# Softmax inverse row sums and output weights of a post-norm transformer block: from TensorE transposes to DMAs

## The reference

```python
x = layernorm(x + attention(x, w_qkv, b_qkv, w_out, b_out))   # 16 heads of width 32, causal softmax
x = layernorm(x + ffn(x))                                      # gate/up/down of width 2048, int weights minus 128, row scales
# attention: softmax(q k^T / sqrt(32) + causal) v, then  out @ w_out.T + b_out
# ffn: Wg = (gate_w - 128) * gate_scale[:, None] and so on;  (silu(x Wg^T) * (x Wu^T)) Wd^T
```

## Time and profile before

| | us |
|---|---|
| three executions: median (lowest, highest) | 734.27 (732.36, 735.01) |
| the profiled execution | 732.33 |
| its span, first to last instruction | 730.5 |
| mean granted TensorE clock, share of full | 0.996 |
| PE busy | 711.2 (97%) |
| DVE, ACT, POOL busy | 386.0, 373.1, 187.0 |

### The profile page before, as it was taken

How to read it: one execution, slowest core, us unless ns; L and a number is a source line. 1 busy time by engine, 2 the same in 40 slices (tenths; PEclk the granted TensorE clock), 3 DMA queues, 4 the chain that set the end, 5 groups by cost and what they waited for, 6 DMA issues and landing times.

```text
span 730.5 us, 11735 instructions
## 1 busy us (share of the span) xinstructions
PE 711.2 (97%) x4368; PEld 551.7 (76%) x4368; DVE 386.0 (53%) x988; ACT 373.1 (51%) x900; POOL 187.0 (26%) x198
## 2 busy tenths in 40 slices
PE   7999899999999999999999999999999999999994
PEld 6777577777777677776688888888888888888883
DVE  4766576666667665577552322553344533544335
ACT  3676676767776776777765653322232222322230
POOL 0011610347132660418833233221020002000004
PEclk9999999999999999999999999999999999999998
DMA  9821453346741577314688964852321013000111
GB/s 306 222 79 30 87 135 126 87 98 143 204 135 59 123 168 235 75 39 116 154 179 162 209 148 145 219 193 79 144 70 45 0 43 129 0 1 1 57 59 59
DMA packets 97207, 83.35 MB, mean 114 GB/s; under 512 B 64128, under 2 KB 73344, under 8 KB 97024
## 3 DMA queue, kind: packets, MB, share of 16 engines
q1 hardware_dynamic: 90624, 62.69, 30.8%
q0 software_dynamic: 6528, 19.93, 12.1%
HBM read 59.53 MB, written 22.02 MB: 112 GB/s over the span
## 4 chain that ended last, share of the span: by engine, by line
PE 92%; POOL 4%; DVE 2%; issue 1%; DMA 1%; ACT 0%; POOLq 0%; SPq 0%; DVEq 0%
PE bank L1506 16%; PE bank L1507 16%; PE bank L1293 12%; PE bank L1372 9%; PE bank L1514 7%; PE bank L1513 7%; PE bank L1311 6%; PE bank L1355 5%; PE bank L1330 5%; PE bank L1393 5%; POOL z_tok L684 1%; PE bank L1404 1%; PE bank L1259 1%; POOL xT_lo L717 1%; DVE probs L1048 1%; POOL z_tok L810 1%
## 5 line engine op out<-in xcount | busy, mean ns | idle before, releaser
L840 ACT ACTIVATE probs<-probs,neg_max 128x128 f32<-128x128 f32 (+3 forms) x256 | 140.3, 552 | 3.0 <-DVE neg_max L1048 2.9
L1048 DVE CUSTOM_DVE_ANT_0 probs<-bank,causal 128x128 f32<-128x128 f32 (+3 forms) x256 | 111.7, 484 | 41.2 <-PE bank L1355 41.2
L1166 DVE SCALAR_TENSOR_TENSOR hid<-bank,u_scale,silu 128x512 f32<-128x512 f32 x64 | 48.0, 750 | 157.2 <-PE bank L1507 156.0
L1506 PE MATMUL bank<-xT_hi,gateT 128*128 128x512 f32 x256 | 99.7, 389 | 0.0
L1507 PE MATMUL bank<-xT_lo,gateT 128*128 128x512 f32 x256 | 99.6, 389 | 0.0
L1506 PE MATMUL bank<-xT_hi,upT 128*128 128x512 f32 x256 | 99.6, 389 | 0.0
L1507 PE MATMUL bank<-xT_lo,upT 128*128 128x512 f32 x256 | 99.6, 389 | 0.0
L1372 PEld LDWEIGHTS bank<-ident,probs 128*128 128x128 f32 x640 | 71.5, 140 | 35.0 <-issue 24.2
L948 ACT ACTIVATE silu<-bank,g_scale 128x512 f32<-128x512 f32 x64 | 44.0, 688 | 102.2 <-PE bank L1507 102.2
L898 ACT ACTIVATE probsT<-bank 128x512 f32<-128x512 f32 x80 | 47.7, 596 | 92.0 <-PE bank L1372 90.1
L954 ACT ACTIVATE hid_hi<-hid 128x512 fp32r<-128x512 f32 x58 | 36.7, 632 | 107.7 <-DVE hid L1166 107.7
(11 more groups left out here) (105 smaller groups left out, 1164.0 us busy)
## 6 DMA issues: line engine op xcount, KB each, us to landing
halves<-x_tok SPq DMA_DIRECT2D x7, 1024.0 KB, 6.4
x_tok<-halves SPq DMA_DIRECT2D x7, 1024.0 KB, 8.2
scan_buf<-in_L_ffn_gate_w_dram SPq DMA_DIRECT2D x4, 1024.0 KB, 6.1
scan_buf<-in_L_ffn_up_w_dram SPq DMA_DIRECT2D x4, 1024.0 KB, 5.4
scan_buf<-in_L_ffn_down_w_dram SPq DMA_DIRECT2D x4, 1024.0 KB, 5.3
w_int<-in_L_ffn_gate_w_dram POOLq DMA_DIRECT2D x16, 256.0 KB, 3.0
w_int<-in_L_ffn_up_w_dram POOLq DMA_DIRECT2D x16, 256.0 KB, 3.2
w_int<-in_L_ffn_down_w_dram POOLq DMA_DIRECT2D x16, 256.0 KB, 4.0
```

The lines of the kernel that those rows point to most:

```text
L840: nc.scalar.activation(probs[qb][:, j, :], probs[qb][:, j, :], ACT.Exp, bias=neg_max[:, qb, j:j + 1], scale=-1.0, accum_out=row_sum[:, qb, ...
L1048: nc.vector.tensor_tensor_reduce(out=probs[qb][:, j, :], in0=score[j][:, first:first + w], in1=causal[:, S - w:S], scale=-SCALE, scalar=-F ...
L1166: nc.vector.scalar_tensor_tensor(out=hid[:, i % 2, :], in0=bank[:, :], scalar=u_scale[:, i:i + 1], in1=silu[:, i % 2, :], op0=ALU.mult, op ...
L1506: nc.tensor.matmul(acc[n][:, :], w[:, c, cols], form(xT_hi[:, c, :]), start=c == 0, stop=False)
```

## The change

Two parts. **Inverses:** DVE writes the reciprocals in a padded layout, transposes them in 32x32 blocks, SP stores them to DRAM (128 rows of 128 B) and loads them back broadcast to 128 partitions of 2 KB (`inv_rows`); `normalise` waits for that load. The second reciprocal moves from step 9 to step 8 (to step 2 in the last group). In the last group ACT issues both DMAs, at steps 2 and 6. POOL's widening, PE's transposes and ACT's copy go. **Output weights:** `w_out` is turned by eight DMA transposes of 2-byte halves in group 0, stored and loaded again in group 1, joined by POOL in group 3, and split into hi (ACT) and lo (POOL) in group 4. The order on SP changes with it: in g = 2 the inverse's two DMAs and the next `load_scan` come ahead of `turn` (behind it in the last batch); in g = 3 the inverse's DMAs come behind the stores, the load of `z_tok` and `store_halves`.

```diff
-    INVERSE_STEP = 15
+    TURN = 32
+    STORE_STEP, SPREAD_STEP = 2, 6
-        (kind, n) for n in range(2, NG) for kind in "qk"] + [("o", n) for n in range(ND)]
+        (kind, n) for n in range(2, NG) for kind in "qk"]
-    W_STEPS = {(0, 4): 8, (0, 7): 9, (1, 4): 10, (1, 7): 11, (3, 4): 12, (3, 6): 13, (4, 4): 14, (4, 6): 15}
+    W_STEPS = {(0, 4): 8, (0, 7): 9, (1, 4): 10, (1, 7): 11}
+    W_OUT_STEPS = [3, 5, 7, 9]
...
-            if s == INVERSE_STEP:
-                banks.whole(("r", G))
...
+        def store_inverse(eng, G):
+            eng.wait_ge(inv_turned_done, G + 1)
+            eng.dma_start(inv_dram.rearrange("j (q a r) -> (j q) a r", a=P // TURN, r=TURN).rearrange("c a r -> a c r"),
+                          inv_turned[:, :]).then_inc(inv_stored, 16)
+
+        def load_inverse(eng, G):
+            eng.wait_ge(inv_stored, 16 * (G + 1))
+            if G > 0:
+                eng.wait_ge(normed, G)
+            eng.dma_start(inv_rows[:, :], inv_dram[:, 0:S].unsqueeze(1).broadcast_to((HG, HD, S))).then_inc(inv_spread, 16)
...
+            def turn_w():
+                for t in range(NT):
+                    wait_full(sp, "w", w_tile("v", t))
+                for e in range(2 * ND):
+                    sp.dma_start(w_place.rearrange("p c (e s) -> p (c e) s", e=2)[:, e, :],
+                                 w_out.bitcast(U16)[:, e * P:(e + 1) * P], transpose=True).then_inc(w_turned, 16)
+            def store_w():
+                sp.wait_ge(w_turned, 16 * 2 * ND)
+                sp.dma_start(w_halves_dram...).then_inc(w_halves_stored, 16)
+            def load_w_halves():
+                sp.wait_ge(w_halves_stored, 16)
+                sp.dma_start(w_place, w_halves_dram...).then_inc(w_halves_loaded, 16)
+            def spread_inverse(G):
+                store_inverse(sp, G)
+                load_inverse(sp, G)
...
-            for i in range(W_PLACES, NW):
-                load_w(i)
             for G in range(GROUPS):
                 b, g = divmod(G, NG)
-                if G in SCAN_GROUPS[1:]:
+                if G in SCAN_GROUPS[1:] and g != 3:
                     load_scan(SCAN_GROUPS.index(G))
...
                 if g == 2:
-                    turn(b + 2)
+                    if b == LAST:
+                        turn(b + 2)
+                    spread_inverse(G)
+                    if G + 1 in SCAN_GROUPS:
+                        load_scan(SCAN_GROUPS.index(G + 1))
+                    if b < LAST:
+                        turn(b + 2)
...
                 if g == 3:
                     store_halves(b + 2)
+                if g != 2 and G < GROUPS - 1:
+                    spread_inverse(G)
+                if G == 0:
+                    turn_w()
+                if G == 1:
+                    store_w()
+                    load_w_halves()
...
-                widen_inverse(G)
+                if G == NG - 1:
+                    join_w()
+                if G == NG:
+                    for c in range(ND):
+                        w_out_lo(c)
...
+                    if s == STORE_STEP and G == GROUPS - 1:
+                        store_inverse(act, G)
+                    if s == SPREAD_STEP and G == GROUPS - 1:
+                        load_inverse(act, G)
...
-                    if s == INVERSE_STEP:
-                        keep_inverse(G)
+                    if G == NG and s in W_OUT_STEPS:
+                        w_out_hi(W_OUT_STEPS.index(s))
...
+            def turn_inverse(G):
+                if G > 0:
+                    dve.wait_ge(inv_stored, 16 * G)
+                wait_alone(dve, inv_done, 2 * (G + 1))
+                nc.vector.transpose(inv_turned[:, :], inv_sum[:, :, :].rearrange("p j q -> p (j q)")).then_inc(inv_turned_done, 1)
             def normalise(G):
-                wait_drained(dve, "r", G)
+                dve.wait_ge(inv_spread, 16 * (G + 1))
+                if G > 0:
+                    dve.wait_ge(att_ready, G)
                 dve.wait_ge(pv_full, G + 1)
-                nc.vector.tensor_tensor(attT[:, :], pv_acc[:, :], attT[:, :], ALU.mult).then_inc(normed, 1)
+                nc.vector.tensor_tensor(attT[:, :], pv_acc[:, :], inv_rows[:, :], ALU.mult).then_inc(normed, 1)
...
-                    if s == 9:
+                    if s == (8 if G < GROUPS - 1 else 2):
                         inverse_sum(G, 1)
+                        turn_inverse(G)
...
-                    for n in range(ND):
-                        wait_drained(pe, "w", w_tile("o", n))
+                    pe.wait_ge(w_out_done, ND)
...
-                    if s == INVERSE_STEP:
-                        last_products = products_at(STEPS) if G == GROUPS - 1 else []
-                        for m in last_products[:-1]:
-                            weighted_values(G, m)
-                        transpose_inverse(G)
-                        for m in last_products[-1:]:
+                    if s == STEPS - 1 and G == GROUPS - 1:
+                        for m in products_at(STEPS):
                             weighted_values(G, m)
```

More of the change, by code:

```diff
@@ L391, in postln_block_kernel @@
         xT_done = sem("xT_done")
+        w_turned = sem("w_turned")
+        w_halves_stored = sem("w_halves_stored")
+        w_halves_loaded = sem("w_halves_loaded")
+        w_joined = sem("w_joined")
+        w_out_hi_done = sem("w_out_hi_done")
+        w_out_done = sem("w_out_done")
         z_loaded = sem("z_loaded")
@@ L509, in load_w @@
             def load_w(i):
[L510 to L514, removed]
+                sp.dma_start(w_stage[:, i, :], w_qkv[w_row(i):w_row(i) + P, :]).then_inc(w_loaded[i], 16)
             def load_x(t):
@@ L529, in _ @@
             sp.dma_start(bias_v[:, :], b_qkv[2 * D:3 * D].partition_broadcast(P)).then_inc(bias_v_loaded, 16)
-            for i in range(8, W_PLACES):
+            for i in range(8, NW):
                 load_w(i)
@@ L835, in next_hi, with w_out_hi @@
                 nc.scalar.activation(xT_hi[:, c, :], x_whole[:, c, :], ACT.Copy).then_inc(x_hi_done, 1)
+            def w_out_hi(c):
+                act.wait_ge(w_joined, c + 1)
+                nc.scalar.activation(wT_hi[:, c, NE:NE + D], w_whole[:, c, NE:NE + D], ACT.Copy).then_inc(w_out_hi_done, 1)
             def exponential(G, qb, j):
@@ L1011, in _ @@
         def _(dve):
+            nc.vector.memset(inv_sum[:, :, :], 0.0)
             nc.vector.memset(ln_stat[:, :, :], 0.0)
@@ L1258, in transpose_weights @@
                 for c in range(ND):
-                    last = nc.tensor.transpose(acc[:, c * P:(c + 1) * P], w_stage[:, w_place(i), c * P:(c + 1) * P], ident[:, :])
+                    last = nc.tensor.transpose(acc[:, c * P:(c + 1) * P], w_stage[:, i, c * P:(c + 1) * P], ident[:, :])
                 last.then_inc(full_of("w", i), 1)
@@ L1397, in weighted_values @@
                     last.then_inc(pv_full, 1)
-            def transpose_inverse(G):
-                acc = bank_for("r", G)
-                pe.wait_ge(inv_widened, G + 1)
-                for qb in range(NT):
-                    last = nc.tensor.transpose(acc[:, qb * P:(qb + 1) * P],
-                                               inv_wide[:, qb, :, :].rearrange("p j d -> p (j d)"), ident[:, :])
-                last.then_inc(full_of("r", G), 1)
             transpose_x(0)
```

48 lines of the change are left out of this document (28 added, 20 removed).

## The result

| us | before | after |
|---|---|---|
| median (lowest, highest), 4 runs each | 734.64 (732.36, 735.49) | 747.26 (745.02, 749.36) |
| ratio after / before, 95% interval | | 1.0158 (1.0119 to 1.0198) |
| the profiled execution | 732.33 | 745.02 |
| its span | 730.5 | 743.2 |
| mean granted clock | 0.996 | 0.984 |

The forecast was 730.1, in a range of 724.5 to 736.6: it is wrong in sign and by 17 us. All the loss is in the attention (12.4 us later at the first gate matmul); the feed-forward takes the same.

A forecast was written before the change was run, and what follows sets the result against it. PE, busy in 97% of the span, was taken to bound the kernel. Terms: -8.9 for removed PE work, +1.4 at groups 7 and 11, +3.3 at the feed-forward's entry: -4.2 from 734.27 gives 730.1 us, range 724.5 to 736.6.

The forecast's parts named there:

- What goes: PE in attention: four transposes per group, 7.0 us over 16 groups, and `w_out` tiles, 1.9 us; together 8.9 us gained.
- 273 ns reading: Rival on PE: each of the 80 removed transposes costs 273 ns, gain 22 us, time 717.2; chance 0.01.
- What comes on DVE, ACT, POOL: New DVE transpose of 0.2 us and split of `w_out` on ACT and POOL fit idle time: nothing, at worst 0.5 us each.
- every pair is late: Rival at `normalise` of 14 ordinary groups: inverse's store and load take 15.4 us, late 0.6 each; 740.2 us, chance 0.11.
- Groups 7 and 11: Late `turn` and `store_halves` on SP delay the inverse; `normalise` late 1.4 to 4.2, PE stalls 0.7 twice: 1.4 us lost.
- The last group: ACT issues both inverse DMAs between exponentials and evictions; in time if they take under 8 us: nothing lost.
- Paid only once: A delay in the last group moves PE towards the late SP, so it is not paid again at the feed-forward.
- Entry of the feed-forward: SP 3.3 us later, PE 0.9 earlier; scales and staged down weights come late: 3.3 us lost, range 2 to 5.
- The turn of batch 0: `turn(2)` waits some 6 us for group 2's inverse, `store_halves(2)` 6 us later in group 3: nothing, at worst 2 us.
- Pile-up: Rival: `normalise` late 4.2 us in groups 8 and 12, group 4 pays 2, feed-forward 5: +2.3, 736.6 us; chance 0.18.

The follow-up runs named there:

- run 2: Kernel before the change with only the output weights moved to DMAs and POOL, inverses and the rest of SP's order as before: 731.08 us, ratio 0.9944.
- Run 4: Changed kernel with useless PE transposes of the identity added in groups 8 and 12 to keep PE busy: 751.32 us, ratio 1.0227.
- run 1: Changed kernel with the inverse's store and load issued in g = 3 ahead of y1 stores, `z_tok` load and `store_halves`: 748.35 us, ratio 1.0170.
- run 10: Changed kernel with `turn` ahead of the scan's load but behind the inverse's store and load in groups 2, 6, 10: 746.93 us, ratio 1.0155.
- run 8: Changed kernel with `turn` ahead of the inverse's DMAs and scan's load in groups 6 and 10, group 15's inverse by PE: 728.16 us, ratio 0.9924.
- run 7: Changed kernel with only the inverses of groups 14 and 15 done by PE as before the change: 742.28 us, ratio 1.0103.
- run 5: Changed kernel with `turn` ahead of the inverse's DMAs and scan's load in groups 6 and 10, all inverses by DMA: 731.12 us, ratio 0.9956.
- run 6: Changed kernel with `turn` first in groups 6 and 10, inverses of groups 14 and 15 widened by POOL and transposed by PE: 728.31 us, ratio 0.9922.
- run 9: Changed kernel with `turn` first in groups 6 and 10, group 15's inverse and the `w_out` tiles by PE: 732.50 us, ratio 0.9946.

## Why the prediction was wrong

The spans differ by +12.7 us where -4.2 was forecast, 16.9 apart. By term: 13.7 are groups 7 and 11 (15.1 against 1.4), 5.8 the last two groups (against nothing), 0.5 what was gained less than forecast, and some 3.0 go the other way at the entry of the feed-forward (0.3 against 3.3).

**What goes: right.** 0.44 us a group and 1.9 us for `w_out`: groups of 21.36 us, 7.6 gained of 8.1 up to `normalise` of group 13, and run 2 alone at -1.6. The price per transpose was taken from the distance between starts, and by the 273 ns reading the groups would have shrunk by 1.1 us, which they didn't. The Trainium skill's rule ("VectorE: DVE Perf Modes", Rules for kernel authors) that 128x128 transposes go to TensorE where PSUM will do is not borne out for the weights' part, faster by 0.25 to 0.86% in run 2: the engine relieved is the full one.

**What comes on DVE, ACT, POOL: right.** The 128x32 transpose takes 0.21 us (0.2 predicted), and ordinary pairs are in time: their stores land in 1.94 to 3.5 us (236.26 to 238.20 and 257.62 to 261.14 in the changed kernel), where 0.4 + 2.5 was taken. The load was mis-sized here too, 4.2 us from its issue against 0.4 + 2.5, at no cost, as the pair had 12 us. The rival "every pair is late" is refuted.

**Groups 7 and 11: the step that failed.** The mechanism and the place were right, the size not. Predicted: 0.7 us each. Measured: 5.7 and 9.4, together 15.1 against 1.4. Term by term for group 7, with the changed kernel's times shifted by the 4.5 us that its groups are earlier:

| term | predicted | measured (shifted) |
|---|---|---|
| `turn(3)` starts | 177.3 | 177.7 |
| it holds SP | 10.3 to 13.7 | 13.9 (group 10's: 16.3) |
| `store_halves(3)` issued | 194.2 to 197 | 196.5 |
| inverse's store landed | 203.1 to 205.9 | 205.4 |
| the load | 0.4 + 2.3 | 5.5 (group 11's: 5.8) |
| `normalise` late by | 1.4 to 4.2 | 6.5 (group 11's: 9.2) |
| PE stands still | 0 to 2.1 | 3.7 (group 12: 5.7) |
| lowered clock | not in the sum | some 2.0 (group 12: 3.7) |

Down to the store's landing the stacking holds. The load was priced near the 2.0 us of another 256 KB transfer, but this one takes 4.2 us with nothing else moving (group 9's), so 1.5 of the 2.8 us that are missing in group 7 are the load itself and not the crowd. The other 1.3 (1.6 in group 11) come with the two 1 MB loads that are issued within 1.1 us behind it; that these delay it is likely but not shown. The upper end of that row would have been the nearer one. `turn(4)` is longer than any `turn` in the rows read. And a PE that has stood still is slow afterwards, which the sum had not at all. PE's idle time and the clock are divided by an estimate from the rows by stretch: idle is what is missing from PE's busy time (3.7 of the 5.7 us lost), and the rest agrees with the work done at a granted clock of 0.50 to 0.93 counted at full speed (1.6 us in 210 to 216 us; 3.7 in group 12). Run 4 was meant to measure this and did not.

The step saw the scan's load too ("late by as much and held by the same stall"), and in the changed kernel that was so: ACT waits for no scan there. What it didn't see is that the scan alone is enough for the stall: in run 1 the inverses are in time there and ACT waits for the scan instead, and in run 10 both wait. The start of `turn(3)` was right, by the scan's load at 176.90, which is the later of the two things ahead of it. The other one is group 6's pair, and run 10 shows that it makes 13.5 of the 16.3 us alone; the earlier trace rows pointed to it with `turn(2)`, which "waits for group 2's inverse, some 6 us".

**The last group: "nothing" was wrong, the second failed step.** It cost 5.8 us, 4.9 net of the transposes. "The inverse can be spread then if the pair takes under 8 us" didn't hold: the pair took 11.1 us from ACT's store to `normalise` (367.13 to 378.24), which waited 2.74 us where it had waited 1.96 before. Some 1.6 us of the cost are again the clock (0.67 in 374 to 376 us, 0.50 in 376 to 378 with PE busy), as an estimate from these stretches. What wasn't asked is what stands behind the two DMA issues and the wait between them on ACT: a table load and evictions for PE (run 8: 3.0 us of it are ACT's pair). "Paid only once" was right: run 7 got 4.9 us back and returned 3.1 at the next place.

**Entry of the feed-forward: right in size, hidden in this kernel, and wrong in its cause.** Predicted +3.3 (2 to 5). In the changed kernel 0.3, as PE comes 12.4 us late. Where the attention is in time it is there, with the waits named: 2.3 (run 5), 2.6 (run 8), 4.2 (run 6), ACT waiting 0.6 to 0.9 for the scales, 3.5 to 3.8 for `down_short`, and PE 1.8 to 2.1. But run 6 pays it with no pair on SP, so the term's cause, SP held 3.3 us by the pair, is not it. In run 8 the pair does hold `load_short(0)` back by 3.0 us (13.69 us from the start of `turn(5)`, 10.73 in run 6), but by the end of the second down weights' issues only 0.6 of that is left (53.9 against 53.3 us). What it is instead stays open: in run 6 SP starts as much earlier as PE, loses about a microsecond over its gapless issues (down weights issued to 381.2, against 387.4), and the last of them land 2 us later after their issue than before.

**The turn of batch 0: right in the time.** The distances into group 4 and the next are 22.54 and 20.18 us, together 2 x 21.36; DVE waited 1.09 us for the inverse once, at no cost. But `turn(2)` held SP 17.9 us instead of 13.7, and `store_halves(2)` was issued at 101.34 against 91.77, 9.6 us later and not 6.

**The chances.** "Pile-up", at 0.18, was the right kind of rival and was priced at +2.3 by adding covers that were all small. Without the two failed terms the forecast's sum came near: run 8, with the order of SP mended and ACT's pair gone, is at 728.2 (ratio 0.9924, -5.6 us), where the sum said -4.2.

## What to carry to other kernels

On a queue that issues its DMAs in program order, as SP here, an inserted small transfer can cost what its wait costs everything behind it: find for each insertion what the wait in front of it is waiting for, and put transfers whose inputs are ready long before (here `turn`) ahead of those whose inputs come last. When a stall moves instead of going away as the order is changed locally, look upstream for the transfer that started late. A wait on an engine's own queue between two of its DMA issues (ACT's pair) is priced by what the engine would have done next, not by the transfer. The version with `turn` first and the last group's inverse on PE beats both kernels, 0.8% faster than the kernel before.

## What the runs showed of the hardware

- After PE had stood still for some microseconds the granted clock fell to half (0.50, that is 1.2 GHz instead of 2.4) and stayed there for a while with PE busy again: 212 to 214 us and 305 to 309 us in the changed kernel, both 1.00 in the kernel before and in run 5, where PE doesn't stand still there. Stalls of 5.7 us in group 12 thus cost 9.4. Shorter pauses went either way: at the entry of the feed-forward the clock fell after 2.09 us (run 6) and 2.77 (run 9), and stayed at 1.00 after 1.75 (run 5), 1.81 (run 8) and 2.76 (run 7).
- Eight DMA transposes of one `turn` held SP 10.2 to 13.9 us in the kernel before (534.72 and 10.90) and up to 17.9 us in the changed one (`turn(2)` at 81.97) and 19.55 in run 9; the number of the instructions is the same.
- The same 16 KB store landed in 1.94 us with nothing else under way, in 4.5 us when two 1 MB transfers had been issued 3.0 and 3.4 us before it (run 5, 188.06 to 192.51, 2.8 us ahead of the second of them), and in 8.35 us behind two 1 MB transfers issued in the microsecond before it.
- The 256 KB broadcast load (128 packets of 2 KB, read from 8 KB of DRAM) took 4.2 us with nothing else under way, at 86 GB/s while its packets moved, where a 256 KB store to `out_dram` lands in 2.0.
